# Attention outputs kept with heads on partitions and normalised in place, instead of turned twice by TensorE

## The reference, cut to what matters

```python
# layer 1 (causal, 8 sequences), x = x + a(layernorm(x))
attn = where(causal, q @ k.T * HD ** -0.5, -inf)
a = clip(attn, -100, 100); m = max(a); e = exp(a - m)
p = e / (sum(e) + 1e-6); p = p + 1e-8; p = p / sum(p)
out = (p @ v).reshape(b, t, c) @ w_proj.T
# layers 2 and 4 (4 x 128 = 512 tokens in each of 8 sequences)
probs = softmax(q @ k.T * HD ** -0.5)
x = layer_norm(src + (probs @ v).reshape(B, T, D) @ Wo + bo)   # then experts
```

## Time and profile before

| | |
|---|---|
| Time, three runs | 2593.06 us median (2582.32 to 2595.44) |
| The profiled execution, its own time | 2579.53 us |
| Its span, first to last instruction | 2577.8 us |
| Granted TensorE clock, mean share of full speed | 0.977 |
| Busy: PE, DVE, ACT, POOL | 2418.6, 1831.9, 1438.2, 1351.5 us |
| Attention over n = 0 to 15 and n = 16 to 23 | about 61 to 1140 us, 1776 to 2295 us of the span |

### The profile page before, as it was taken

The page is one execution under the profiler, slowest core; times in us unless marked ns, Lnnn a source line. Parts: engine busy times, 40 slices in busy tenths (PEclk is TensorE's granted clock), DMA queues, the critical chain, the costliest instruction groups (busy, mean ns, idle before and its releaser), DMA issues. The chain is left out here.

```text
span 2577.8 us, 45874 instructions
## 1 busy us (share of the span) xinstructions
PE 2418.6 (94%) x14724; PEld 1393.9 (54%) x14724; DVE 1831.9 (71%) x3685; ACT 1438.2 (56%) x2991; POOL 1351.5 (52%) x1358
## 2 busy tenths in 40 slices
PE   6999999999999999989999699988999999989998
PEld 3455555554444444349899366653344434349997
DVE  5999999999778888854333558867778888845333
ACT  3666666666777777753333232214777777653332
POOL 5356666563234554444655579843334454435655
PEclk8999999999999999999999799988999999999999
DMA  5333333333434444324665200015434444335654
GB/s 161 101 105 107 105 102 108 112 105 96 120 112 124 133 129 125 98 93 161 213 201 179 72 1 17 17 58 138 118 109 129 129 130 122 85 118 176 202 194 141
DMA packets 249936, 305.88 MB, mean 119 GB/s; under 512 B 28034, under 2 KB 224865, under 8 KB 249700
## 3 DMA queue, kind: packets, MB, share of 16 engines
q1 hardware_dynamic: 238164, 275.37, 35.8%
q0 software_dynamic: 10176, 26.27, 2.9%
q10 hardware_dynamic: 1360, 1.31, 0.2%
HBM read 210.32 MB, written 92.84 MB: 118 GB/s over the span
## 5 line engine op out<-in xcount | busy, mean ns | idle before, releaser
L783 DVE TENSOR_REDUCE neg_max_af<-sc_af 128x1 f32<-128x512 f32 (+3 forms) x864 | 551.0, 664 | 105.2 <-PE sc_af L489 101.2
L704 ACT ACTIVATE prob_af<-sct_af 128x512 f32<-128x512 f32 (+1 forms) x864 | 484.1, 582 | 234.9 <-PE sct_af L512 231.3
L783 DVE TENSOR_REDUCE neg_max_f<-sc_f 128x1 f32<-128x512 f32 x512 | 334.6, 685 | 93.0 <-PE sc_f L489 90.8
L704 ACT ACTIVATE prob_f<-sct_f 128x512 f32<-128x512 f32 x512 | 290.6, 598 | 127.5 <-PE sct_f L512 126.1
L512 PE MATMUL sct_af<-stack_q_af,stack_k_af 99*128 99x512 bf16 (+3 forms) x1024 | 320.1, 343 | 7.9 <-ACT prob_af L704 7.1
L489 PE MATMUL sc_af<-stack_k_af,stack_q_af 96*128 96x512 bf16 (+3 forms) x1024 | 320.0, 342 | 4.1 <-DVE neg_max_af L783 4.0
L1620 PE MATMUL y_ps_e<-w_r,hT_e 128*128 x1120 | 255.4, 381 | 5.7 <-issue 4.0
L812 DVE SCALAR_TENSOR_TENSOR prob_af<-prob_af,w_r 128x512 f32<-128x512 f32 (+2 forms) x224 | 233.2, 1049 | 21.7 <-ACT prob_af L704 21.5
L1807 DVE TENSOR_TENSOR y_e<-y_ps_e,b_e 128x256 f32<-128x256 f32 x70 | 29.7, 425 | 298.3 <-PE y_ps_e L1620 296.5
L540 PE MATMUL out_af<-prob_af,v_aug_af 128*32 128x512 f32 (+3 forms) x2048 | 231.9, 525 | 8.7 <-DVE prob_af L812 7.8
L1620 PEld LDWEIGHTS y_ps_e<-w_r,hT_e 128*128 128x128 f32 x1120 | 207.2, 190 | 35.3 <-issue 9.4
(11 more groups left out here) (383 smaller groups left out, 4650.0 us busy)
## 6 DMA issues: line engine op xcount, KB each, us to landing
w_r<-in_f_W_dram SPq DMA_DIRECT2D x66, 1024.0 KB, 5.1
stack_k_af<-k_parts_d SPq DMA_DIRECT2D x64, 384.0 KB, 4.3
k_parts_d<-parts_af SPq DMA_DIRECT2D x187, 128.0 KB
q_parts_d<-parts_af SPq DMA_DIRECT2D x96, 128.0 KB
stack_q_af<-q_parts_d SPq DMA_DIRECT2D x64, 192.0 KB, 2.9
stack_k_f<-k_parts_d SPq DMA_DIRECT2D x32, 384.0 KB, 4.2
w_next<-in_f_W_dram SPq DMA_DIRECT2D x12, 1024.0 KB, 4.9
k_parts_d<-parts_f SPq DMA_DIRECT2D x91, 128.0 KB
```

The lines of the kernel that those rows point to most:

```text
L704: nc.scalar.activation(dst, src.rearrange("p (h q) -> p h q", h=len(heads)), ACT.Exp).then_inc(S.exp_done, 1)
L783: nc.vector.tensor_reduce(M.neg_max[:, qt, heads[0]:heads[-1] + 1], src, AX.X, ALU.max, negate=True).then_inc(S.max_done, 1)
```

## The change

- The outputs of a group stay as `pv` makes them, a head's channels on partitions. `move_out` (SP) issues five transfers: the four heads' sums into `sums`, 32 to a partition, and four blocks of 16 rows from `o_sb` to their place in `attT[n % 2]`. The transposes of outputs and of `attT`, and ACT's copies of `attT`, go.
- For each half of a sequence (two groups), DVE works out the factors on 128 x 32 numbers (`weigh`, in the slot kt = 3), SP stores them to DRAM (`store_weights`) and loads them back with each head's row repeated over 16 partitions (`spread_weights`), and POOL multiplies (`scale_out`; causal: multiplies, scales the floor's share, adds). The first half is scaled in the next sequence.
- The second half of sequences 14, 15, 22 and 23 (`by_pe`) still goes by PE.
- The rows of maxima are turned by one transpose of 48 columns, not four of 12; they leave as 48 pieces of 256 bytes, not 12 of 1 KB. The sum over v is made as two columns.
- SP: `load_max_rows(n, 3)` moves ahead of `save_src` and `load_x`; the new transfers stand behind rows of maxima or ahead of and behind a `load_stack`.
- Semaphores are merged in the small chains of POOL (`inv_std`), with the same waits.

```diff
@@ light_at, closing
-        elif kt == 2:
+        elif kt == 2 and by_pe(group(n, g - 1)[0], group(n, g - 1)[1] // 2):
             use = ("out",) + group(n, g - 1)
-        elif s in attT_slots(n):
+        elif s == 3 and exists(n - 1) and by_pe(n - 1, 1):
...
@@ sync
+            def move_out(n, g):
...
+                c, h = divmod(g, 2)
+                sp.wait_ge(S.o_sb, NG * n + g + 1)
+                if n > 1:
+                    sp.wait_ge(S.y_ps, 2 * (n - 1))
...
+                sp.dma_start(M.sums[64 * h:64 * h + 64, :], M.o_sb[HD:P:32, :]).then_inc(S.moved, 16)
+                for i in range(4):
+                    o = 64 * h + HD * i
+                    sp.dma_start(M.attT[n % 2][o:o + HD, c, :], M.o_sb[32 * i:32 * i + HD, :]).then_inc(S.moved, 16)
...
+            def spread_weights(n, c):
...
+                sp.wait_ge(S.weights_stored, 16 * spreads(n, c))
+                sp.wait_ge(S.moved, 80 * moved(n, 2 * c + 1))
...
+                for at in range(2 if causal(n) else 1):
+                    sp.dma_start(M.spread[:, at, :], M.weights_d[n % NB][at, hs, :].unsqueeze(1).to_broadcast([8, HD, T])).then_inc(S.weights_spread, 16)
...
                 load_stack(n, 3)
                 load_max_rows(n, 1)
+                move_out(n - 1, 3)
                 load_res(n - 1)
                 write_parts(n + 1, 0)
+                store_weights(n - 1, 1)
                 load_stack(n + 1, 0)
+                spread_weights(n - 1, 1)
                 load_max_rows(n, 2)
+                move_out(n, 0)
                 write_parts(n + 1, 1)
                 load_stack(n + 1, 1)
+                load_max_rows(n, 3)
+                move_out(n, 1)
                 save_src(n + 2)
                 load_x(n + 3)
-                load_max_rows(n, 3)
+                store_weights(n, 0)
                 load_stack(n + 1, 2)
+                spread_weights(n, 0)
                 if exists(n - 1) and not ffn(n - 1):
                     store(n - 1)
                 load_max_rows(n + 1, 0)
+                move_out(n, 2)
@@ tensor
-                    for t in range(KT):
-                        last = nc.tensor.transpose(Gb[0:12, t * P:t * P + P], M.max_parts[:, t, :, :].rearrange("p a h -> p (a h)"), C.ident_bf[:, :])
+                    last = nc.tensor.transpose(M.gen_bf[bank_of[use]][0:12 * KT, 0:P], M.max_parts[:, :, :, :].rearrange("p a h t -> p (a h t)"),
+                                               C.ident_bf[:, :])
@@ vector
+            def weigh(n, c):
...
+                dve.wait_ge(S.moved, 80 * moved(n, 2 * c + 1))
...
+                    nc.vector.tensor_scalar(M.e8[:, :], M.sums[:, :], 1e-6, 1e-8, ALU.add, ALU.mult).then_inc(S.norm_step, 1)
...
+                    nc.vector.reciprocal(M.weights[:, 0, :], M.sums[:, :]).then_inc(S.weighed, 1)
...
+                        if kt == 3 and pg % 2 == 1:
+                            weigh(pn, pg // 2)
@@ gpsimd
+            def scale_out(n, c):
...
+                pool.wait_ge(S.weights_spread, 16 * spreads(n, c))
+                out = M.attT[n % 2][:, c, :]
+                if causal(n):
+                    pool.wait_ge(S.v_all, n + 1)
...
+                    nc.gpsimd.tensor_tensor(out, out, M.spread[:, 0, :], ALU.mult).then_inc(S.floor_v, 1)
+                    nc.gpsimd.tensor_scalar(M.spread[:, 1, :], M.spread[:, 1, :], M.v_all[:, n % 2, c:c + 1], None, ALU.mult).then_inc(S.floor_v, 1)
...
+                    nc.gpsimd.tensor_tensor(out, out, M.spread[:, 1, :], ALU.add).then_inc(S.attT_ready, 1)
+                else:
+                    nc.gpsimd.tensor_tensor(out, out, M.spread[:, 0, :], ALU.mult).then_inc(S.attT_ready, 1)
...
                 lay_out_v(n, 3)
+                scale_out(n - 1, 0)
                 split(n + 1, 1)
                 split(n + 1, 2)
-                add_floor(n - 1, 3)
                 split(n + 1, 3)
                 inv_std_x(n + 2)
-                add_floor(n, 0)
+                scale_out(n - 1, 1)
                 add_bias(n - 1)
```

More of the change, by code:

```diff
@@ L72, in y_slot, with by_pe, moved, outs @@
         return 4 if n == end - 1 else 8
-    def attT_slots(n):
-        return (3, 4) if n == end - 1 else (4, 7)
+    def by_pe(n, c):
+        return c == 1 and n >= NB and n % NB >= NB - 2
+    def moved(n, g):
+        return sum(1 for m in range(n + 1) for q in range(NG) if (m, q) <= (n, g) and not by_pe(m, q // 2))
+    def outs(n, g):
+        return NG * n + g + 1 - moved(n, g)
+    def pe_chunks(n):
+        return outs(n, NG - 1) // 2
+    def chunks(n, c):
+        return moved(n, 2 * c + 1) // 2
+    def spreads(n, c):
+        return chunks(n, c) + min(chunks(n, c), 2 * NB)
     first_ffn = max(first, NB)
@@ L215, in attention @@
                   ("max", first, 0), ("qk", first + 1, 2), ("qk", first + 1, 3)])
-    closing = [("out", last, NG - 1), ("attT", last, 0), ("attT", last, 1), ("y", last, 0), ("y", last, 1)]
+    closing = [("out", last, NG - 1), ("attT", last, 1), ("y", last, 0), ("y", last, 1)]
     bank_of, used_before = {}, {}
@@ L402, in bank_free @@
                     what, m, j = used_before[use]
[L403 to L404 removed]
+                    if what == "out":
+                        pe.wait_ge(S.out_read, 2 * outs(m, j))
+                    elif what == "attT":
+                        pe.wait_ge(S.attT_copied, pe_chunks(m))
+                    else:
+                        per, sem = READ_OUT[what]
+                        pe.wait_ge(sem, per * read_count(what, m) + j + 1)
             def use_bank(use, halves=(0, 1)):
@@ L668, in read_bank @@
                         act.wait_ge(S.max_rows[pg], 16 * (pn + 1))
-                    nc.scalar.activation(M.max_sb[:, j % 2, :], M.gen_bf[bank_of[use]][0:12, 0:T], ACT.Copy).then_inc(S.max_sb, 1)
+                    nc.scalar.activation(M.max_sb[:, j % 2, :], M.gen_bf[bank_of[use]][0:12 * KT, 0:P], ACT.Copy).then_inc(S.max_sb, 1)
             def read_qk(use, full):
@@ L768, in _ @@
             read_out(last, NG - 1)
-            for use in closing[1:3]:
-                read_bank(use)
+            read_bank(closing[1])
         @block.vector
@@ L1219, in _ @@
                 scatter(n - 2)
+            scale_out(last, 0)
             add_bias(last)
```

199 lines of the change are left out of this document (104 added, 95 removed).

## The result

The changed kernel takes 2642.69 us (median of 4 runs, 2636.32 to 2649.69), the kernel before, run beside it, 2590.18: ratio 1.0202, 95% interval 1.018 to 1.0224. It is slower by 2%, where 3.5% faster was forecast. In the profiled executions the span grows from 2577.8 to 2634.6 us, by 56.8.

A forecast was written before the change was run, and what follows sets the result against it. PE was taken as the bound, with DVE nearly full in the causal layer. Savings of 58 us (second and fourth layers) plus 24 (causal) gave 82 off 2579.5, 2497.5; plus 6 for the median, 2503 us, range 2470 to 2560.

The forecast's parts named there:

- Light uses: Second-layer slots with PE transposes (outputs, `attT`, maxima) take 0.42 to 0.44 us extra; removal saves 3.9 us a sequence.
- near 3.8: Sign expected in the second layer: slots kt = 1, with rows of maxima, fall to about 3.8 us.
- Late sequences: Sequences 11 to 13 and 19 to 21: POOL's chain sets the start of s = 2, leaving 3.7 us gain each.
- I take nothing, and keep 16 x 2.4 = 38 us as the other end: Second and fourth layers: POOL's new products colliding with DVE's casts priced at zero, 38 us as the other bound.
- DVE's slack: Second layer: DVE has 11 us or more to spare in a sequence, so collisions with POOL were charged nothing.
- Causal layer: Gross gain 5.5 us a sequence less 2.5 charged: net 3.0, or 24 us over 8 sequences; bounds 0 and 44.
- I charge 2.5 us in all: Causal sequence: total cost of the later k parts and rows of maxima, the next sequence's first rows included.
- 1.3 of 3.7 us: Causal third group's rows of maxima: delay behind 512 KB of spread factors, taken as 1.3 from 0 to 3.7 us.
- New transfers: SP: 26 new issues of 0.6 us, 16 us a sequence, fit its 35 us of causal waits; no cost charged.
- a sign of being wrong: The prediction would be wrong if `weigh` waits for DMA, SP has no waits left, or moves exceed 1.2 us.
- The rival with SP as the bound: SP's issues set the pace: 2660 us at 1.5 us a move, 2600 at 1.3; chance 0.12.
- the one in which GpSimd stops VectorE and the causal gain is gone: 38 us lost and no causal gain, or `weigh` waits for sums: 2567 to 2593 us, within 0.5%; chance 0.08.

The follow-up runs named there:

- run 7: Changed kernel with causal rows of maxima ahead of the spreads, and `add_bias` ahead of the second half's `scale_out` in second and fourth layers: 2574.01 us, 0.9952.
- run 13: Causal layer as before the change; second and fourth layers changed, `add_bias` ahead of `scale_out`, second half's factor spread ahead of the stack: 2559.11 us, 0.9888.
- run 14: Run 13 with the three operations of `scale_y` each cut into two of 128x512: 2556.22 us, 0.9878.
- run 15: Run 13 with the operations of `scale_y` cut into quarters of 128x256: 2543.27 us, 0.9835.
- run 3: Changed kernel with causal rows of maxima (third group, next sequence's first group) issued ahead of the spreads of factors: 2599.18 us, 1.0039.
- run 10: Run 7 with the floor factor's product by the sum of v made as a product with a broadcast tensor: 2577.10 us, 0.9978.
- run 11: Run 10 with the first half's `scale_out` ahead of the layout of v for the fourth group, causal layer: 2561.46 us, 0.9915.
- run 17: Changed kernel in all layers with every repair: reordered rows, spreads, `scale_out` and `add_bias`, broadcast floor product, `scale_y` and splits in 128x256 operations: 2522.51 us, 0.9791.
- run 2: Changed kernel with each spread of factors bringing 16 columns instead of 512, except in each call's first sequence: 2571.10 us, 0.9944.
- the cut alone: Kernel before, without the change, with GpSimd's `scale_y` and splits in operations of 128x256: 2572.51 us, 0.9953.

## Why the prediction was wrong

**Light uses.** Right in kind. Slots kt = 2 are 3.71 us as forecast, kt = 1 3.98 instead of "near 3.8": one transpose of 48 columns saves 0.15 us of a slot and not three quarters of 0.42. The single one still costs the slot 3.98 - 3.71 = 0.27 us, the other three only 0.15 together. An early sequence gives 3.7 us and not 4.5, where four slots kt = 1 lack 0.7 and s = 8 the rest.

**Late sequences.** Forecast 3.7 us less each, measured 0.3 (n = 10 to 13) and 1.0 (18 to 21) more in the mean. The step that failed is "I take nothing, and keep 16 x 2.4 = 38 us as the other end". I priced a collision as the new product meeting a cast. What costs is that the product, with its wait for the spread in front, shifts everything that GpSimd does behind it: `scale_y` moved by 4.0 us in the sequence, and by 5.5 against PE's slots, which had become shorter. So it stands in VectorE's split of the maxima, where each small operation can wait for 2.2 us of GpSimd. Runs 7, 13, 14 and 15 show both halves, the shift and the wait for a whole operation; run 13 shows that the shorter slots and the product are enough without the wait. DVE's slack, on which I rested, does not help, since PE waits for this very piece of its work. The 1.5 us at s = 9 are not followed here; they are gone in run 7 (3.98).

The Trainium skill (GPSIMD Engine Reference, Key points) has the rule that GpSimd contends with VectorE's 2-port modes and two-input operations. The runs agree, with a price that this section does not give: up to one whole operation of GpSimd for each small one of VectorE. By that rule I had worked out 38 us as an end and set it aside.

**Causal layer.** Forecast 3.0 us less each, measured 6.5 more in the mean of the eight (8.1 by the medians of n = 1 to 7, 69.8 to 77.9). The step that failed is "I charge 2.5 us in all". It had the queue too small, and had no term for the splits meeting VectorE's split of the maxima:
- The queue. Rows behind the spread need 5.4 to 5.6 us from issue to use, 3.0 with the rows in front (run 3). That is 2.4 to 2.6 us at each of two places; I took 1.3 of 3.7 us at one, and let the second, the next sequence's first rows, go into the same 2.5 us. It happened at s = 5 or 6 and at s = 14, and at s = 14 there was no slack. With the clock behind it, it costs 6.2 us a sequence (medians of n = 1 to 7, 77.9 to 71.7, run 3). The part behind it that is clock is not separated: rows show s = 15 at 0.50 taking 3.1 us more, no run holds the clock still.
- The collision. k parts left 4.7 us later in their sequence (11.2 to 15.9 us after its start; forecast 4), as said, but the floor row's wait was 1.06 us of the stop. The rest was VectorE, held by splits that came late: two casts cost 1.7 us more than alone and `weigh` 1.4, and the clips, behind both on DVE, held PE for another 2.12 us. With the rows ahead, s = 5 is still 10.2 - 4.5 = 5.7 us too long. I had not followed the splits' end, only k's, and had counted `weigh` as 0.9 us of DVE without asking what stands behind it. Each reordering moved this stop: s = 5 (runs 3, 10), s = 1 (run 11). Cutting the operations made it smaller (run 17).

The Trainium skill (DMA: Bandwidth & Descriptors, Two DMAs through the same engine are not ordered) says that descriptors in one queue start in order; by that I had the full 3.7 us as a stall and weighed it away. Runs 2 and 3 side with the rule, at 2.4 to 2.6 us.

**New transfers.** Right in size: a move takes 0.59 us of SP in the median (4 of 352 over 1.2), SP still waits 247.5 us for rows of maxima in the first two layers, `weigh` waits for moves twice in the whole program, 3.5 us each, which the prediction had named as a sign of being wrong. The rival with SP as the bound was not it. The rival that came true is the one in which GpSimd stops VectorE and the causal gain is gone, and I ended it at 2593 us because I took it for no worse than the gains.

**Size.** Of the forecast's 82 us about two thirds were there under the stops. With all repairs the sequences 8 to 14 give 23 us, 16 to 22 21 us, the causal ones 16 us (24 were forecast for them); of these 60 us 5 to 8 are those of the cut alone. What is left of the causal shortfall stays open: s = 1 and s = 5 are still 5.7 and 5.3 us, where 4.5 was before.
